# Where Q's block forms of x and V's first group of forms are made, in a fused cross-attention and expert kernel

## The chip, the core and the metric

The kernel runs on one NeuronCore of a Trainium2 chip. The metric is the device time of one execution in microseconds, median of several. TensorE (PE) multiplies matrices, VectorE (DVE), ScalarE (ACT) and GpSimd (POOL) work elementwise, SyncE (SP) issues the transfers here. GpSimd does not touch PSUM in this kernel.

## The reference

```python
def _layernorm(x): return (x - mean(x)) / sqrt(var(x) + 1e-5)

def xattn(h, ctx, mask, bias, ln_weight, w_q, w_k, w_v, w_out):   # 32 heads of 128
    x = rmsnorm(h) * ln_weight
    q, k, v = x @ w_q.T, ctx @ w_k.T, ctx @ w_v.T                 # 1024 x 512 @ 512 x 4096 each
    p = softmax(where(mask, q @ k.T + bias, -inf))                # per head and batch, 128 x 128
    return h + (p @ v) @ w_out.T

x = x + tanh(g_xattn) * xattn(layernorm(x), ctx_4096, ...)
x = x + tanh(g_ffn) * ffn(layernorm(x), ...)                      # base product, top 2 of 28 rank-8 experts
```

x and the context are 8 x 128 x 512 in float32.

## The kernel before

**Precision.** A float32 matrix is split into a rounded part `hi` (float32r, written by ScalarE, the "lead") and the rest `lo` = raw - hi (written by VectorE or GpSimd). Each product is three matmuls: hi x hi, hi x lo, lo x hi.

**Stages.** (1) The context is split, K and V of the first head pair are made, x is normalised and turned, and Q of the first pair is made. (2) `q_phase(0)` to `q_phase(14)`: Q of the other 15 head pairs. (3) V of the other 15 pairs, in four groups `g` of 4, 4, 4 and 3 pairs. (4) Attention over the pairs, with K made on the way. (5) The expert layer.

**Block products.** Stages 2, 3 and K use a scheme of 7 half-size products in place of 8. For Q the weights give the forms A11, A12, A22 (blocks as they are) and S1 to S4 (sums of blocks), x gives the blocks B11, B21, B22 and four forms T1 to T4, which are made once, before phase 0, and serve all 15 phases:

T1 = B12 - B11, T2 = B22 - T1, T4 = B21 - T2, T3 = B22 - B12.

In the code T1 to T4 are `t_raw[0]` to `t_raw[3]`. `t_form` on VectorE (line 1226) makes them, `lead_t` (854) rounds them on ScalarE, `rest_t` (1231) makes their rests on VectorE. The products of a phase stand on TensorE in this order: A11 B11; S1 T1; A12 B21; A22 T4; S2 T2; S4 B22; S3 T3. Each is 6 matmuls of 512 columns (line 1810). `post` on VectorE (1259) adds the products up; the seventh needs the post of the fifth, since it takes that bank again. `rest_a` (1236) makes the rests of A on VectorE; the sums S (`s_forms`, lines 600 to 605) and their rests (610) are GpSimd's.

**x before phase 0.** TensorE turns the eight row tiles of x into PSUM (`turn_xn`), ScalarE rounds each (`lead_xt`, 794), VectorE makes the rest (`rest_xt`, 1163), and ScalarE copies the raw tile to SBUF (`raw_xt`, 789). T1 needs both halves of x as raw copies, so VectorE waits for all eight (`xt_raw_done`).

**V's first group.** V's blocks of weights come in four raw slots R11, R21, R22, R12. Seven forms are rounded and multiplied in the order n = 0 to 6 by `v_product` (line 1885, 24 matmuls each, four row tiles of the context). The sums are made in the raw slots themselves:

```python
R11 = R11 - R21        # form 5         v_sums 1   DVE L1270
R21 = R21 + R22        # form 1         v_sums 2   DVE L1273
R21 = R22 - R11        # form 4         v_sums 3   POOL L700
R12 = R12 - R21        # form 3         v_sums 4   POOL L703
```

Form 1 lies where form 4 is written, so form 4 waits for form 1's rest, which is GpSimd's in the first group (`v_on_pool`), as is the rest of form 2 (line 685). The four forms of the context (`kt_raw`, differences at line 1279) are made during the last Q phases; GpSimd makes the rests of two (633, 639), VectorE of the other two (1324). After its sums GpSimd adds mask and bias (`add_mask(0)`, 574) and goes on to group 1. SP loads the blocks of group 1 when the rests of forms 3 to 6 are made.

Everything is a static order per engine with semaphores; each engine works its own list from the top.

## Time and profile before

| | |
|---|---|
| median of 3 runs | 848.75 us (848.27 to 848.85) |
| the profiled execution | 850.35 us, its span 848.6 us |
| busy: TensorE / VectorE / ScalarE / GpSimd | 821.9 / 594.8 / 380.5 / 442.6 us |
| mean granted TensorE clock | 0.991 of full |
| transferred | 145.48 MB, 171 GB/s on average |

The span runs from the first to the last instruction of the profiled execution. Busy time of TensorE includes modelled ends of pipelined matmuls, so starts are the better measure of its pace. In the timeline each row is one instruction or a run of like ones: start, time, engine, line, operation, tiles written and read; in brackets the idle time of the engine before it and what ended that.

### The profile page before, as it was taken

What the parts mean: (1) busy time and instruction counts of PE and PEld (TensorE: products, weight loads), DVE (VectorE), ACT (ScalarE), POOL (GpSimd) and SP (SyncE); (2) the same over time, 40 slices, a digit from 0 to 9 for tenths busy, and PEclk for the clock granted to TensorE, in tenths of its full rate; (3) what the DMA queues carried; (4) which work ended last, traced back from release to release, by engine and by line L of the source; (5) the groups of instructions that cost most, each with busy time, mean ns of one, the idle gap of its engine ahead of it and who ended that gap; (6) DMA issues with size and microseconds to landing.
All of it is one profiled execution on the core that took longest, in us unless ns stands there. A gap on an engine that the chain in (4) does not pass through costs nothing.

```text
span 848.6 us, 14325 instructions
## 1 busy us (share of the span) xinstructions
PE 821.9 (97%) x4270; PEld 702.8 (83%) x4270; DVE 594.8 (70%) x999; ACT 380.5 (45%) x1046; POOL 442.6 (52%) x406
## 2 busy tenths in 40 slices
PE   8979999999999999969999999999999999998998
PEld 6868888877788889858888888888888888887886
DVE  6886555767736354747887779777887788779852
ACT  5554444443433424443456344644555345642410
POOL 1365666676475473547545764477446754571200
PEclk9999999999999999969999999999999999999999
DMA  8228444543635554665665456555655566544001
GB/s 305 93 81 272 166 161 149 174 161 99 199 110 189 174 198 156 216 219 156 220 220 183 155 204 223 203 150 190 239 197 180 172 220 221 191 159 154 1 25 74
DMA packets 78556, 145.48 MB, mean 171 GB/s; under 512 B 7872, under 2 KB 44736, under 8 KB 76608
## 3 DMA queue, kind: packets, MB, share of 16 engines
q1 hardware_dynamic: 78528, 145.12, 50.7%
q8 instruction: 15, 0.25, 0.1%
q14 instruction: 13, 0.11, 0.1%
HBM read 94.77 MB, written 50.33 MB: 171 GB/s over the span
## 4 chain that ended last, share of the span: by engine, by line
PE 84%; DVE 6%; DMA 3%; issue 2%; POOL 2%; ACT 2%; SPq 1%; DVEq 0%; POOLq 0%; ACTq 0%
PE proj_ps L1810 16%; PE proj_ps L1618 13%; PE proj_ps L1866 12%; PE proj_ps L1885 7%; PE score_ps L1618 7%; PE proj_ps L1686 4%; PE score_ps L1885 4%; PE score_ps L1655 3%; PE proj_ps L2051 3%; PE turn_ps L1866 2%; PE pv_ps L1866 2%; PE pv_ps L1885 2%; PE turn_ps L1885 2%; PE score_ps L1686 2%; PE turn_ps L1655 2%
## 5 line engine op out<-in xcount | busy, mean ns | idle before, releaser
L574 POOL TENSOR_TENSOR comb<-mask_add,bias_sb 128x1024 f32<-128x1024 f32 x32 | 77.3, 2438 | 163.7 <-DVE attn L1380 163.7
L778 ACT ACTIVATE attn<-attn,neg_max 128x128 f32<-128x128 f32 x256 | 99.2, 391 | 34.9 <-DVE neg_max L1369 34.9
L984 ACT ACTIVATE w_hi<-w_raw 128x256 fp32r<-128x256 f32 x105 | 39.8, 413 | 102.9 <-POOL w_raw L648 70.0
L1402 DVE TENSOR_TENSOR acc<-proj_ps,acc 128x512 f32<-128x512 f32 x70 | 48.3, 689 | 37.3 <-PE proj_ps L1618 37.3
L658 POOL TENSOR_TENSOR w_lo<-w_raw,w_hi 128x256 fp32r<-128x256 f32 x105 | 73.4, 742 | 0.0
L610 POOL TENSOR_TENSOR w_lo<-w_raw,w_hi 128x256 fp32r<-128x256 f32 x60 | 47.4, 796 | 27.2 <-ACT w_hi L849 27.2
L1618 PE MATMUL proj_ps<-w_hi,tf_hi 128*128 128x512 f32 x156 | 61.1, 392 | 0.4 <-DVE tf_lo L1398 0.4
L1618 PE MATMUL proj_ps<-w_lo,tf_hi 128*128 128x512 f32 x156 | 60.7, 389 | 0.0
L1618 PE MATMUL proj_ps<-w_hi,tf_lo 128*128 128x512 f32 x156 | 60.7, 389 | 0.0
L1264 DVE TENSOR_TENSOR w_lo<-w_raw,w_hi 128x1024 fp32r<-128x1024 f32 (+1 forms) x20 | 28.2, 1426 | 41.0 <-ACT w_hi L884 41.0
L884 ACT ACTIVATE w_hi<-w_raw 128x1024 fp32r<-128x1024 f32 (+1 forms) x28 | 27.6, 1014 | 57.3 <-POOL w_raw L694 21.3
L563 POOL TENSOR_TENSOR w_lo<-w_raw,w_hi 128x1024 fp32r<-128x1024 f32 x20 | 47.6, 2387 | 8.1 <-ACT w_hi L758 8.0
L1686 PE MATMUL proj_ps<-attn,v_sb 128*128 128x128 f32 x376 | 46.5, 282 | 5.4 <-DMA attn<-block_spill 3.6
L1236 DVE TENSOR_TENSOR w_lo<-w_raw,w_hi 128x256 fp32r<-128x256 f32 x45 | 33.8, 755 | 25.4 <-ACT w_hi L844 25.2
L1686 PEld LDWEIGHTS proj_ps<-attn,v_sb 128*128 128x128 f32 x376 | 44.9, 198 | 5.7 <-DMA attn<-block_spill 3.7
L1398 DVE TENSOR_TENSOR tf_lo<-proj_ps,tf_hi 128x512 fp32r<-128x512 f32 x47 | 32.0, 690 | 24.0 <-ACT tf_hi L784 22.0
L778 ACT ACTIVATION_READ_ACCUMULATOR attn<-attn,neg_max 128x1 f32 x256 | 48.6, 190 | 0.0
L1380 DVE TENSOR_TENSOR attn<-attn,row_scale 128x512 f32<-128x512 f32 x64 | 44.3, 692 | 2.2
L1369 DVE TENSOR_REDUCE neg_max<-attn 128x4 f32<-128x512 f32 x64 | 43.9, 686 | 2.2
L849 ACT ACTIVATE w_hi<-w_raw 128x256 fp32r<-128x256 f32 x60 | 24.8, 417 | 42.0 <-PE proj_ps L1810 38.6
L685 POOL TENSOR_TENSOR w_lo<-w_raw,w_hi 128x1024 fp32r<-128x1024 f32 (+1 forms) x8 | 18.5, 2322 | 46.1 <-ACT w_hi L884 44.9
L1866 PE MATMUL proj_ps<-ct_hi,w_hi 128*128 128x512 f32 x90 | 36.8, 409 | 3.1 <-DVE tf_lo L1398 3.1
(326 smaller groups left out, 2542.4 us busy)
## 6 DMA issues: line engine op xcount, KB each, us to landing
w_raw<-in_weights SPq DMA_DIRECT2D x52, 512.0 KB, 5.5
v_sb<-v_spill SPq DMA_DIRECT2D x32, 512.0 KB, 3.7
q_spill<-attn SPq DMA_DIRECT2D x60, 256.0 KB, 3.0
qt<-q_spill SPq DMA_DIRECT2D x15, 1024.0 KB, 4.8
block_spill<-block_sb SPq DMA_DIRECT2D x30, 512.0 KB, 3.5
attn<-block_spill SPq DMA_DIRECT2D x120, 128.0 KB, 2.9
w_raw<-in_v_weights SPq DMA_DIRECT2D x12, 512.0 KB, 4.8
v_spill<-v_sb SPq DMA_DIRECT2D x12, 512.0 KB, 4.6
```

The costliest lines, as they stand in the source:

```text
L563: pool.tensor_tensor(lo, w_raw[:, k, :], hi.bitcast(F32), ALU.subtract).then_inc(w_lo_done[k], 1)
L574: pool.tensor_tensor(comb[:, j, :, :], mask_add[:, :, :], bias_sb[:, j:j + 1, :].to_broadcast([P, B, S]), ALU.add).then_inc(comb_done, 1)
L610: pool.tensor_tensor(columns(w_lo, WO, n), columns(w_raw, s_raw(i), n), columns(w_hi, WO, n).bitcast(F32), ALU.subtract).then_inc(qs_lo, 1)
L658: pool.tensor_tensor(columns(w_lo, slot, n), raw, columns(w_hi, slot, n).bitcast(F32), ALU.subtract).then_inc(k_lo, 1)
L778: e = act.activation(probs[:, u, i, :], probs[:, u, i, :], ACT.Exp, bias=neg_max[:, u, i:i + 1], accum_out=row_sum[:, u, i:i + 1])
L1380: dve.tensor_tensor(probs[:, u, :, :], probs[:, u, :, :], row_scale[:, u, :].unsqueeze(2).to_broadcast([P, BU, S]), ALU.mult).then_inc(pro ...
L1402: dve.tensor_tensor(acc[:, b, :], out_banks[b][:, :], acc[:, b, :], ALU.add).then_inc(acc_done, 1)
L1618: mm = pe.matmul(o, lhs(l, n), rhs(r, n), start=(start and n == 0 and m == 0), stop=(stop and n == terms - 1 and m == 2))
L1686: mm = pe.matmul(pv_bank(a, u)[:, i * S:(i + 1) * S], v_sb[:, b, j * DH:(j + 1) * DH], probs_t[:, t, :, j * BU + i, :], start=True, stop=True)
L1810: mm = pe.matmul(o[:, :], w[l][:, c, :], x[r][:, c, :], start=(start and c == 0 and m == 0), stop=(c == 1 and m == 2), skip_group_check=no ...
L1866: mm = pe.matmul(o[:, :], w[l][:, c, :], x[r][:, c, :], start=(start and c == 0 and m == 0), stop=(c == 1 and m == 2), skip_group_check=no ...
L1885: mm = pe.matmul(banks[m][:, 0:VN[g]], x[l][:, c, m * P:(m + 1) * P], w, start=(start and c == 0 and n == 0), stop=(c == 1 and n == 2), sk ...
```

## The change

**Q's forms of x.** `raw_xt` copies only the first four tiles (the first half of x). T1 and T2 are made tile by tile, four instructions of 128 x 256 each, with the second half of x read straight from the PSUM banks of `turn_xn`. T3 is rewritten from T2 - B11 and T4 from B21 - T2, both from SBUF and whole. T3's difference is made right behind the first rest of A, its lead goes in front of phase 0 on ScalarE. T1's rest goes in front of A's first rest. `T_DONE` holds the new counts.

**V's first group.** Form 1 gets a buffer of its own, `v_first_s1` (the first half of `block_sb`, free once the first context form's rest is made), so form 4 no longer waits for it. VectorE alone makes the sums and the rests of forms 0 to 4, in the order in which the products take them. GpSimd has nothing of group 0 left; its mask addition goes behind group 1's sums. On ScalarE the lead of the context form 1 goes one product earlier, V's form 1 behind the context form 3.

```diff
+T_DONE = (G, 2 * G, 2 * G + 2, 2 * G + 1)
...
+        def v_form_raw(g, n):
+            return v_first_s1 if g == 0 and n == 1 else v_raw(g, V_RAW[n])
+        def v_sum_at(g, n):
+            return g * SF + ({1: 1, 5: 2, 4: 3, 3: 4} if g == 0 else {5: 1, 1: 2, 4: 3, 3: 4})[n]
...
+        v_first_s1 = block_sb[:, 0, 0:2 * VN[0]]
...
         def v_on_pool(g, n):
-            return n == 1 or (n == 0 and g > 0) or (n == 2 and g == 0)
+            return g > 0 and n < 2
...
# GpSimd
             rest_kt(1, 2)
-            v_rest(0, 1)
-            v_rest(0, 2)
-            v_second_sums(0)
-            pool.wait_ge(kt_lo_done, TF)
-            pool.wait_ge(mask_done, 1)
-            add_mask(0)
             for g in range(1, VG):
                 v_rest(g, 0)
                 v_first_sums(g)
                 v_rest(g, 1)
                 v_last_sums(g - 1)
                 v_second_sums(g)
+                if g == 1:
+                    pool.wait_ge(kt_lo_done, TF)
+                    pool.wait_ge(mask_done, 1)
+                    add_mask(0)
...
# ScalarE
             copy_proj(0, UNITS + 4, 1, q_at(1))
-            for i in range(G, B):
-                raw_xt(i)
...
             lead_s(0, 0)
+            lead_t(0)
             copy_proj(0, UNITS + 5, 2, q_at(2))
-            lead_t(0)
+            lead_t(1)
             lead_s(0, 1)
             lead_s(0, 3)
             act.wait_ge(proj_done, PROJ0 - 1)
             lead_a(0, 0, 0, 0)
-            lead_t(1)
             lead_t(3)
             lead_a(0, 1, 0, 1)
-            lead_s(0, 2)
             copy_proj(0, UNITS + 6, 0, q_at(3))
             lead_a(0, 2, 1, 1)
+            lead_s(0, 2)
+            act.wait_ge(proj_done, PROJ0)
+            lead_t(2)
...
                 copy_product(i, s_copy, p1_ps)
+                if last:
+                    lead_kt(1, 3)
...
                 if first:
                     copy_proj(0, PROJ0 - 1, 3, v_dst(3))
                     lead_a(1, 0, 0, 0)
-                    lead_t(2)
...
                 if last:
-                    lead_kt(1, 3)
                     lead_kt(2, 3)
                     product(i, 4)
                     v_lead(0, 0)
-                    v_lead(0, 1)
                     product(i, 6)
                     lead_kt(3, 4)
+                    v_lead(0, 1)
                     product(i, 7)
                     v_lead(0, 2)
...
# VectorE
-            dve.wait_ge(xt_raw_done, B)
-            t_form(0, b_block(0, 1), b_block(0, 0))
-            dve.wait_ge(t_done, 1)
-            t_form(1, b_block(1, 1), t_raw[0])
-            dve.wait_ge(t_done, 2)
-            t_form(3, b_block(1, 0), t_raw[1])
+            dve.wait_ge(xt_raw_done, G)
+            for i in range(G, B):
+                t_tile(0, i, tile_ps(i, 0), tile_of(xt_raw[:, 0:2, :], i))
+            for i in range(G, B):
+                dve.wait_ge(t_done, i - G + 1)
+                t_tile(1, i, tile_ps(i, 1), tile_of(t_raw[0], i))
+            dve.wait_ge(t_done, 2 * G)
+            dve.tensor_tensor(t_raw[3], xt_raw[:, 2:4, half(0)], t_raw[1], ALU.subtract).then_inc(t_done, 1)
+            rest_t(0, 1)
             rest_a(0, 0, 0, 0)
-            rest_t(0, 1)
+            dve.tensor_tensor(t_raw[2], t_raw[1], xt_raw[:, 0:2, half(0)], ALU.subtract).then_inc(t_done, 1)
             rest_a(0, 1, 0, 1)
             rest_a(0, 2, 1, 1)
             rest_t(3, 3)
             rest_t(1, 2)
-            t_form(2, b_block(1, 1), b_block(0, 1))
             rest_t(2, 4)
...
+            def v_first_s1_sum():
+                dve.wait_ge(kt_lo_done, 1)
+                dve.wait_ge(vw_in[R21], 16)
+                dve.wait_ge(vw_in[R22], 16)
+                dve.tensor_tensor(v_first_s1, v_raw(0, R21), v_raw(0, R22), ALU.add).then_inc(v_sums, 1)
+            def v_first_group():
+                v_rest(0, 1)
+                ...
+                dve.tensor_tensor(v_raw(0, R11), v_raw(0, R11), v_raw(0, R21), ALU.subtract).then_inc(v_sums, 1)
+                ...
+                dve.tensor_tensor(v_raw(0, R21), v_raw(0, R22), v_raw(0, R11), ALU.subtract).then_inc(v_sums, 1)
+                v_rest(0, 2)
+                ...
+                dve.tensor_tensor(v_raw(0, R12), v_raw(0, R12), v_raw(0, R21), ALU.subtract).then_inc(v_sums, 1)
+                v_rest(0, 3)
+                v_rest(0, 4)
...
                 if last:
                     v_rest(0, 0)
-                    v_first_sums(0)
+                    v_first_s1_sum()
...
             q_phase(NQ - 1)
+            v_first_group()
...
# TensorE
-                v_product(g, 0, VB["11"], vx_ps, True, posted(g - 1, 13) if g else lambda m: pe.wait_ge(xt_raw_done, B))
+                v_product(g, 0, VB["11"], vx_ps, True, posted(g - 1, 13) if g else lambda m: pe.wait_ge(t_done, T_DONE[1]))
```

**First place: VectorE between the rests of x and phase 0's rests.** In these rows `comb` holds T1 and T2, `attn` the raw x with T3 and T4, `tf_lo` the rests of T1 and T2, and `w_lo<-attn` those of T3 and T4. Before:

```order
L1226 TENSOR_TENSOR comb<-attn 128x1024
L1226 TENSOR_TENSOR comb<-attn,comb 128x1024
L1226 TENSOR_TENSOR attn<-attn,comb 128x2x512
L1236 TENSOR_TENSOR w_lo<-w_raw,w_hi 128x256
L1231 TENSOR_TENSOR tf_lo<-comb,tf_hi 128x1024
L1236 TENSOR_TENSOR w_lo<-w_raw,w_hi 128x256 x2
L1231 TENSOR_TENSOR w_lo<-attn,w_hi 128x1024
L1231 TENSOR_TENSOR tf_lo<-comb,tf_hi 128x1024
L1226 TENSOR_TENSOR attn<-attn 128x2x512
L1231 TENSOR_TENSOR w_lo<-attn,w_hi 128x1024
L1236 TENSOR_TENSOR w_lo<-w_raw,w_hi 128x256 x2
```

After:

```order
L1235 TENSOR_TENSOR comb<-score_ps,attn 128x2x128 x2
L1235 TENSOR_TENSOR comb<-turn_ps,attn 128x2x128
L1235 TENSOR_TENSOR comb<-pv_ps,attn 128x2x128
L1235 TENSOR_TENSOR comb<-score_ps,comb 128x2x128 x2
L1235 TENSOR_TENSOR comb<-turn_ps,comb 128x2x128
L1235 TENSOR_TENSOR comb<-pv_ps,comb 128x2x128
L1255 TENSOR_TENSOR attn<-attn,comb 128x2x512
L1240 TENSOR_TENSOR tf_lo<-comb,tf_hi 128x1024
L1245 TENSOR_TENSOR w_lo<-w_raw,w_hi 128x256
L1258 TENSOR_TENSOR attn<-comb,attn 128x2x512
L1245 TENSOR_TENSOR w_lo<-w_raw,w_hi 128x256 x2
L1240 TENSOR_TENSOR w_lo<-attn,w_hi 128x1024
```

Two wide differences have become eight small ones that read PSUM, T1's rest stands in front of A's first rest, and T3's difference has moved from the last place but one to the place behind it.

**Second place: VectorE from the last Q phase to V's first group.** The rows with `proj_ps` are posts, `w_lo` rests of V's forms, `w_raw` and `block_sb` sums, `xt_lo` the context rests. Before:

```order
L1259 TENSOR_TENSOR attn<-proj_ps,lnw 128x512
L1264 TENSOR_TENSOR w_lo<-w_raw,w_hi 128x1024
L1270 TENSOR_TENSOR w_raw<-w_raw 128x1024
L1273 TENSOR_TENSOR w_raw<-w_raw 128x1024
L1259 TENSOR_TENSOR attn<-proj_ps,attn 128x512
L1259 TENSOR_TENSOR attn<-proj_ps,lnw 128x512
L1259 TENSOR_TENSOR attn<-proj_ps,attn 128x512
L1259 TENSOR_TENSOR attn<-attn 128x512
L1324 TENSOR_TENSOR xt_lo<-comb,xt_hi 128x2x512
L1324 TENSOR_TENSOR xt_lo<-block_sb,xt_hi 128x2x512
L1264 TENSOR_TENSOR w_lo<-w_raw,w_hi 128x1024 x4
```

After:

```order
L1275 TENSOR_TENSOR w_lo<-w_raw,w_hi 128x1024
L1282 TENSOR_TENSOR block_sb<-w_raw 128x1024
L1270 TENSOR_TENSOR attn<-proj_ps,attn 128x512
L1270 TENSOR_TENSOR attn<-proj_ps,lnw 128x512
L1270 TENSOR_TENSOR attn<-proj_ps,attn 128x512
L1270 TENSOR_TENSOR attn<-attn 128x512
L1275 TENSOR_TENSOR w_lo<-block_sb,w_hi 128x1024
L1289 TENSOR_TENSOR w_raw<-w_raw 128x1024
L1291 TENSOR_TENSOR w_raw<-w_raw 128x1024
L1275 TENSOR_TENSOR w_lo<-w_raw,w_hi 128x1024
L1295 TENSOR_TENSOR w_raw<-w_raw 128x1024
L1275 TENSOR_TENSOR w_lo<-w_raw,w_hi 128x1024 x2
```

The first sum is form 1's, in its own buffer; behind the posts follow the other sums and the rests of forms 1 to 4, and the two context rests come only then.

**The same place on GpSimd.** Before:

```order
L639 TENSOR_TENSOR xt_lo<-comb,xt_hi 128x2x512
L685 TENSOR_TENSOR w_lo<-w_raw,w_hi 128x1024 x2
L700 TENSOR_TENSOR w_raw<-w_raw 128x1024
L703 TENSOR_TENSOR w_raw<-w_raw 128x1024
L574 TENSOR_TENSOR comb<-mask_add,bias_sb 128x1024 x2
L685 TENSOR_TENSOR w_lo<-w_raw,w_hi 128x1024
L691 TENSOR_TENSOR w_raw<-w_raw 128x1024
L694 TENSOR_TENSOR w_raw<-w_raw 128x1024
```

After:

```order
L647 TENSOR_TENSOR xt_lo<-comb,xt_hi 128x2x512
L693 TENSOR_TENSOR w_lo<-w_raw,w_hi 128x1024
L699 TENSOR_TENSOR w_raw<-w_raw 128x1024
L702 TENSOR_TENSOR w_raw<-w_raw 128x1024
L693 TENSOR_TENSOR w_lo<-w_raw,w_hi 128x1024
L718 TENSOR_TENSOR attn<-attn,k_buf 128x512 x4
L708 TENSOR_TENSOR w_raw<-w_raw 128x1024
L711 TENSOR_TENSOR w_raw<-w_raw 128x1024
L582 TENSOR_TENSOR comb<-mask_add,bias_sb 128x1024 x2
```

Two rests and two sums of group 0 are gone, and the two mask additions (`comb<-mask_add,bias_sb`) stand behind group 1's sums.

## Rows read from the trace of the kernel before

**Rows 1.** The page, part 1: busy us (share of the span) xinstructions

```profile
PE 821.9 (97%) x4270; PEld 702.8 (83%) x4270; DVE 594.8 (70%) x999; ACT 380.5 (45%) x1046; POOL 442.6 (52%) x406
```

**Rows 2.** Waits of TensorE, 40 to 66 us: total us, times, longest

```profile
PE proj_ps L1810 <- DVE attn L1259: 3.4, 1, 3.4
```

**Rows 3.** The same view, 180 to 220 us

```profile
PE proj_ps L1885 <- DVE w_lo L1264: 1.7, 1, 1.7
...
PE proj_ps L1885 <- issue: 0.6, 1, 0.6
```

**Rows 4.** Timeline of TensorE: start us, us, engine line op tiles [idle before <-releaser]

```profile
47.00 0.28 PE L1618 MATMUL proj_ps<-w_lo,ct_hi 128*128 128x256 f32 x1
...
48.00 0.50 PE L1810 MATMUL proj_ps<-xt_hi,w_hi 128*128 128x512 f32 x1 [0.72 <-DVE w_lo L1236]
...
60.73 0.47 PE L1810 MATMUL proj_ps<-w_hi 128*128 128x512 f32 x1 [3.42 <-DVE attn L1259]
...
62.17 0.39 PE L1810 MATMUL proj_ps<-xt_hi,w_hi 128*128 128x512 f32 x1
...
196.43 0.42 PE L1885 MATMUL score_ps<-w_hi,ct_hi 128*128 128x512 f32 x1
...
221.07 0.39 PE L1885 MATMUL score_ps<-w_hi,xt_hi 128*128 128x512 f32 x1
```

**Rows 5.** Window sums: stretch, length, then PE, PEld, DVE, ACT, POOL, clock, DMA

```profile
61.00:185.00 124.00, 124.00 (x546) 102.03 (x544) 77.74 (x109) 57.38 (x130) 79.88 (x102) 1.00 0.54 181
```

**Rows 6.** Timeline of VectorE, 40 to 61 us

```profile
42.49 1.23 DVE L1226 TENSOR_TENSOR comb<-attn 128x1024 f32<-128x1024 f32 x1 [2.49 <-ACT attn L789]
...
52.48 1.75 DVE L1231 TENSOR_TENSOR tf_lo<-comb,tf_hi 128x1024 fp32r<-128x1024 f32 x1
...
58.17 1.81 DVE L1236 TENSOR_TENSOR w_lo<-w_raw,w_hi 128x256 fp32r<-128x256 f32 x2
...
60.51 0.41 DVE L1236 TENSOR_TENSOR w_lo<-w_raw,w_hi 128x256 fp32r<-128x256 f32 x1
```

**Rows 7.** Timeline of ScalarE, 45 to 50 us

```profile
45.89 0.42 ACT L844 ACTIVATE w_hi<-w_raw 128x256 fp32r<-128x256 f32 x1 [0.46 <-PE proj_ps L1618]
...
49.20 0.40 ACT L844 ACTIVATE w_hi<-w_raw 128x256 fp32r<-128x256 f32 x1
...
49.70 0.60 ACT L891 ACTIVATE lnw<-proj_ps 128x512 f32<-128x512 f32 x1
```

**Rows 8.** Timeline of GpSimd, 49 to 53 us

```profile
49.85 0.74 POOL L600 TENSOR_TENSOR w_raw<-w_raw 128x256 f32<-128x256 f32 x1 [0.17 <-POOL w_lo L610]
...
51.43 1.71 POOL L603 TENSOR_TENSOR w_raw<-w_raw 128x256 f32<-128x256 f32 x1
```

**Rows 9.** Timeline of VectorE, V's first and second group

```profile
194.01 0.69 DVE L1259 TENSOR_TENSOR attn<-proj_ps,lnw 128x512 f32<-128x512 f32 x1 [4.91 <-PE proj_ps L1810]
...
196.41 1.23 DVE L1270 TENSOR_TENSOR w_raw<-w_raw 128x1024 f32<-128x1024 f32 x1
...
203.01 3.42 DVE L1324 TENSOR_TENSOR xt_lo<-comb,xt_hi 128x1024 fp32r<-128x1024 f32 x1
...
251.45 1.23 DVE L1264 TENSOR_TENSOR w_lo<-w_raw,w_hi 128x1024 fp32r<-128x1024 f32 x1 [10.96 <-ACT w_hi L884]
```

**Rows 10.** Timeline of ScalarE, V's form 3

```profile
212.05 1.06 ACT L884 ACTIVATE w_hi<-w_raw 128x1024 fp32r<-128x1024 f32 x1 [8.15 <-POOL w_raw L703]
```

**Rows 11.** Timeline of GpSimd, V's groups

```profile
205.31 3.37 POOL L700 TENSOR_TENSOR w_raw<-w_raw 128x1024 f32<-128x1024 f32 x1
...
211.97 5.72 POOL L574 TENSOR_TENSOR comb<-mask_add,bias_sb 128x1024 f32<-128x1024 f32 x2
...
263.66 2.41 POOL L685 TENSOR_TENSOR w_lo<-w_raw,w_hi 128x1024 fp32r<-128x1024 f32 x1 [13.39 <-ACT w_hi L884]
```

**Rows 12.** w_raw between 186 and 204 us: loads (ns min/median/max, starts), landing

```profile
L339 SPq DMA_DIRECT2D w_raw<-in_v_weights x2: 400/1495/2590, 189.6 to 190.0; - x2
...
DMA to landing us min/median/max: 5.3/5.7/6.1
```

More of the change, by code:

```diff
@@ L1219, in _, with tile_ps, tile_of, t_tile @@
                 rest_xt(i, xt_hi_done, xt_lo_done, xn_ps)
-            def b_block(k, t):
-                return xt_raw[:, 2 * k:2 * k + 2, half(t)]
-            def t_form(n, l, r, op=ALU.subtract):
-                dve.tensor_tensor(t_raw[n], l, r, op).then_inc(t_done, 1)
+            def tile_ps(i, k):
+                return xn_ps[i % G][:, 2 * k * P:(2 * k + 2) * P].rearrange("p (c s) -> p c s", c=2)
+            def tile_of(raw, i):
+                return raw[:, :, (i - G) * P:(i - G + 1) * P]
+            def t_tile(n, i, l, r):
+                dve.tensor_tensor(tile_of(t_raw[n], i), l, r, ALU.subtract).then_inc(t_done, 1)
             def rest_t(n, place):
@@ L1336, in v_group @@
             def v_group(g):
-                for n in range(2 if g else 3, VFORMS):
+                for n in range(2 if g else 5, VFORMS):
                     v_rest(g, n)
```

29 lines of the change are left out of this document (13 added, 16 removed).

## The prediction

> **What bounds the kernel now.** I read the page first: TensorE is busy for 821.9 us of the 848.6 us span [rows 1]. So time can come only out of TensorE's gaps, and a change that touches VectorE, ScalarE and GpSimd is worth what it does to those gaps. Next I read who makes TensorE wait, in the two stretches that the diff touches. Around the first block phase of Q TensorE stands for 3.4 us and for 0.7 us, both times for VectorE [rows 2, 4]. Where V's first group begins it stands for 1.7 us behind a VectorE rounding rest and for 0.6 us that the view calls "issue" [rows 3]; that product waits for GpSimd's rest of form 1 by the code, so I count it as GpSimd's. Between the two, 546 matmuls fill 124.00 us without a gap, 0.227 us each, at the full granted clock [rows 5], so neither a clock step nor a hidden wait is to be had there.
>
> The modelled ends of matmuls hide part of a gap, so I price gaps by starts. First place: the last matmul of V's last row block starts at 47.00, the 256 columns cost 0.12 us, and phase 1 of Q starts at 62.17 [rows 4]. 42 matmuls of phase 0 need 42 x 0.227 = 9.5 us; 62.17 - 47.12 - 9.5 = 5.5 us are lost. Second place: V's first product starts at 196.43, the fifth at 221.07 [rows 4]. 96 matmuls need 21.8 us of the 24.64; 2.85 us are lost. The two places together, 8.4 us, are all that this change can win.
>
> **Part 1, Q's forms of x.** Before, VectorE idles 2.49 us before T1's difference at 42.49, because that waits for ScalarE's four copies of the second half of x; it had been free since 40.0 [rows 6]. Afterwards those four copies are gone (about 2 us of ScalarE, off the path) and T1 and T2 are built tile by tile from PSUM. That is 8 instructions of 256 elements. No such instruction is in the trace. The nearest is the 256-element rest of 0.41 us [rows 6]; back to back a start follows the last one some 0.08 us before its end, so 0.34 us each, 2.7 us in all, from 40.0 to 42.7. Bounds: 0.33 and, if each were as slow as in the blocked pair (1.81 us for two [rows 6]), 0.9 us, which would end at 47.1.
>
> Then T4's difference and T1's rest follow, wide ones of 1.23 us alone [rows 6], 1.14 us from start to start: done at 45.0. A11's rest now stands behind them, and its lead cannot begin before 45.89, when TensorE has read Q's old weights [rows 7]. Lead 0.42, rest 0.41: 46.75. TensorE is free at 47.12, so the 0.7 us wait goes.
>
> ScalarE's list from 45.89 to the copy at 49.70 is the same seven kinds of instruction as before (T3's lead in the place of T2's), so the copy that frees the first bank begins at 49.20 + 0.33 = 49.5 and ends at 50.1 [rows 7]. TensorE's third product could start at 49.85; it starts at 50.2, a new wait of 0.35 us. Its seventh product is then due at 50.2 + 4 x 1.36 = 55.65, against 60.73 before [rows 4].
>
> **What is late next** is VectorE. Between A11's rest and the seventh product it still has T3's difference, two rests of A, three rests of T, two rests of A for phase 1 and one addition. Alone that is 1.14 + 0.66 + 3.42 + 0.66 + 0.7 = 6.6 us, from 46.7 to 53.3, early enough. It isn't alone. A wide VectorE instruction at 52.48 took 1.75 us where an undisturbed one takes 1.23, and the GpSimd instruction beside it (256 wide, 51.43) took 1.71 where its fellows need 0.74 [rows 6, 8]: the two take turns, and each GpSimd instruction costs VectorE about 1.75 - 1.23 = 0.52 us. In this stretch GpSimd has the last rest of S, four sums for phase 1 and a rest, and five to six of them fall between: 3.0 us, an estimate from these rows. So the addition ends at 56.3 and the seventh product starts at 56.35. **Gain 60.73 - 56.35 = 4.4 us.** Bounds: 5.1 us if VectorE is not the limit (55.65), and 2.6 us if every instruction of that list is as slow as its blocked fellow before (1.7 wide, 0.9 narrow: 11.8 us from 46.3, 58.15). I take 4.4, because the count of GpSimd instructions is known and the 0.52 us is what the rows show for each.
>
> The Trainium skill's page "SBUF — State Buffer", section "Who interferes with whom", says that a VectorE instruction with two SBUF inputs and a GpSimd instruction that reads SBUF exclude each other for the whole of whichever starts first. Taken at its worst (VectorE always just too late, 0.74 us each, six times) it makes the loss 4.4 us, the seventh product 57.7 and the kernel 1.4 us slower than my number, an estimate by that page. By the same section an instruction with one input from PSUM is not in this at all; no row here shows eight such tiles beside GpSimd.
>
> **Part 2, V's first group.** All times here are of the old trace; the shift from part 1 moves every engine alike. Before, VectorE and GpSimd blocked each other: the two rests of KT took 3.42 us instead of 1.23 [rows 9], GpSimd's sum 3.37 us at 205.31 [rows 11], and ScalarE waited 8.15 us for the sum chain before it could make form 3 [rows 10]. Afterwards GpSimd has nothing ready after KT's second rest until group 1's data is in, so VectorE's wide instructions cost 1.23 us.
> - S1 into its own buffer needs R22. Its load is issued by 190.0 and lands at most 6.1 us later, 196.1 [rows 12]. Form 0's rest begins after the addition at 194.01 [rows 9] and ends at 195.9. S1: 196.1 to 197.35 (1.23 as at 196.41 [rows 9]). ScalarE leads it by 198.4 (1.06 [rows 10]).
> - Four additions of 0.61 us follow on VectorE, to 199.8; S1's rest is ready at 201.0. TensorE wants it at 196.43 + 24 x 0.227 = 201.87. Margin 0.9 us; the 0.6 us wait goes.
> - Two differences, form 2's rest, S4's difference: about 1.23 each, ready at 203.6, 204.8, 206.0. TensorE wants form 2 at 207.3: margin 2.5 us.
> - ScalarE's form 3 at 206.1 to 207.1, its rest at 208.3. TensorE wants it at 212.8. Margin 4.5 us; the 1.7 us wait goes.
> - What moves: lead of KT's form 1 goes one product earlier on ScalarE and delays one copy by 0.1 us with 3 us of room. The two KT rests come after form 4, at 211 to 214; they are first wanted after 223. SP's loads for group 1 hang on the rests of forms 3 to 6 and go out some 4 us earlier, so they cost nothing. The mask addition (two instructions, 5.72 us [rows 11]) goes behind group 1's sums. It then runs where GpSimd idled for 13 us, and may block group 1's form 3 on VectorE by 2.3 us, against a margin that I put at 2.9 us: before, this rest ended at 252.7 [rows 9], 1.0 us before TensorE wanted it (221.07 + 6 x 5.44 = 253.7), and the chain to it starts 4.5 us earlier now, TensorE only 2.7. So nothing, with an upper bound of 1 us.
>
> **Gain 2.85 us**; bounds 1.8 (that 1 us) and 2.85, since there is no more gap to take.
>
> **Sum.** 4.4 + 2.85 = 7.25 us. The profiled execution took 850.35 us around its span of 848.6; it would become 843.1 around 841.35. The median of the three runs is 848.75, 1.6 us below the profiled one, and gives 841.5. 0.2% (1.7 us) is about what a measurement tells from no change.
>
> **The rivals.**
> - *V's sums still come late.* VectorE does nine wide instructions one behind the other. If R22 lands late or the four additions wait, S1's rest misses 201.87. For it: the margin is only 0.9 us. Against it: all later margins are over 2 us. Only the first gain stays: 848.75 - 4.4 = 844.3. 8%.
> - *Q's gain is given back.* Phase 0 ends earlier, but the next weights, the ring of stores or GpSimd's sums don't, and a phase soon after waits. Against it: phases 1 to 12 ran without a gap on weights that came a phase ahead. 848.75 - 2.85 = 845.9. 8%.
> - *Blocking in both places, slower.* If GpSimd always had an instruction ready, all VectorE instructions of V's chain would cost 3.42 us like KT's rests [rows 9]. From 199.8: S1's rest at 203.2 (1.3 late), form 2's rest at 213.5 (4.9 more), form 3's at 221.4 (2.5 more), 8.7 us of gaps for 2.85, with 2.6 in part 1: 848.75 + 5.85 - 2.6 = 852.0. New gaps appear once a step takes over 1.9 us (7.5 us for four), and the whole turns slower from 2.9 us a step. Against it: GpSimd's list is empty there. 3%.
> - *It doesn't do what it says*: TensorE waits for another thing at both places, and nothing changes, 848.75. Every wait named has its releaser in the views. 3%.
>
> **The numbers.** The forecast, 841.5, has 78%. Its own ends are 4.4 to 8.4 us of gain (2.6 + 1.8 to all of both gaps), 844.4 to 840.35. The range 840.2 to 844.8 takes in the first rival and leaves out 14%. Faster by over 0.2%: 0.94; within: 0.03; slower: 0.03.
>
> **What would show it.** T1's first tile starts at about 39.9 and T2 ends by 43; TensorE's phase 0 starts at 47.1; its seventh product waits under 1 us for the same addition and starts at 56 to 56.7. VectorE's wide instructions between 190 and 210 (less the shift of 4.4) show 1.23 us and GpSimd none beside them; TensorE has no gap over 0.1 us from V's first product on. VectorE at 1.7 us or more there, or a gap in front of V's second product, would make the second part wrong; a seventh product after 57.5 the first.

## The result and the profile after

| | before | after |
|---|---|---|
| median of the runs, us | 848.51 (848.25 to 848.85, 4 runs) | 840.98 (840.78 to 842.29, 4 runs) |
| profiled execution, us | 850.35 (span 848.6) | 840.79 (span 839.0) |
| ratio after / before | | 0.9901, 95% interval 0.9888 to 0.9915 |

The change makes the kernel faster. The median after is 0.5 us under the forecast of 841.5; the ratio, which compares runs of one chip, makes the gain 8.4 us of 848.5 (7.2 to 9.5), where the two places were to give 7.25. A second comparison of the same kernel, `both` below, gave 0.9895. So the sign and the places came as forecast, and the gain is about 1 us more than the sum.

TensorE's busy time on the page answers to [rows 1]: 821.9 us became 819.3 us, while the span fell by 9.6.

```profile
PE 819.3 (98%) x4270; PEld 703.2 (84%) x4270; DVE 589.7 (70%) x1009; ACT 380.1 (45%) x1042; POOL 429.6 (51%) x402
```

TensorE's waits from 36 to 66 us after the change, in place of [rows 2]:

```profile
PE proj_ps L1644 <- DVE xt_lo L1169: 0.3, 1, 0.3
PE proj_ps L1836 <- ACT lnw L897: 0.2, 1, 0.2
```

And its timeline, in place of [rows 4]:

```profile
45.84 0.28 PE L1644 MATMUL proj_ps<-w_lo,ct_hi 128*128 128x256 f32 x1
45.96 0.40 PE L1836 MATMUL proj_ps<-xt_hi,w_hi 128*128 128x512 f32 x1
...
49.06 0.47 PE L1836 MATMUL proj_ps<-xt_hi,w_hi 128*128 128x512 f32 x1 [0.20 <-ACT lnw L897]
...
54.63 0.47 PE L1836 MATMUL proj_ps<-w_hi 128*128 128x512 f32 x1
...
56.10 0.39 PE L1836 MATMUL proj_ps<-xt_hi,w_hi 128*128 128x512 f32 x1
...
190.22 0.39 PE L1911 MATMUL score_ps<-w_hi,ct_hi 128*128 128x512 f32 x1
...
195.66 0.39 PE L1911 MATMUL proj_ps<-w_hi,xt_hi 128*128 128x512 f32 x1
...
211.98 0.39 PE L1911 MATMUL score_ps<-w_hi,xt_hi 128*128 128x512 f32 x1
```

Read by starts, as the prediction did. From V's last projection to phase 1: 56.10 - 45.84 - 9.65 = 0.6 us lost, 5.5 before. From V's first product to its fifth: 21.76 us for 96 matmuls, nothing lost, 2.85 before. That is 4.9 + 2.85 = 7.8 us. The remaining 1.8 us of the difference of spans lie in code that the change does not touch: the last projection began 1.16 us earlier, the fourteen phases between, 1 to 14, were 0.14 us shorter and all behind V's fifth product 0.5 us.

VectorE after the change, in place of [rows 6]:

```profile
39.74 0.42 DVE L1235 TENSOR_TENSOR comb<-pv_ps,attn 128x256 f32<-128x256 f32 x1
40.07 0.75 DVE L1235 TENSOR_TENSOR comb<-score_ps,comb 128x256 f32<-128x256 f32 x2
...
48.69 1.75 DVE L1240 TENSOR_TENSOR tf_lo<-comb,tf_hi 128x1024 fp32r<-128x1024 f32 x1
50.37 1.76 DVE L1240 TENSOR_TENSOR w_lo<-attn,w_hi 128x1024 fp32r<-128x1024 f32 x1
52.05 1.83 DVE L1245 TENSOR_TENSOR w_lo<-w_raw,w_hi 128x256 fp32r<-128x256 f32 x2
53.80 0.68 DVE L1270 TENSOR_TENSOR attn<-proj_ps,lnw 128x512 f32<-128x512 f32 x1
```

The reader sees the eight tiles at 0.33 us from start to start, T1 and T2 done at 41.5, and the addition for the seventh product done at 54.48, 0.15 us before TensorE starts it. VectorE and TensorE arrive together there. V's first group, in place of [rows 9]:

```profile
189.53 1.22 DVE L1282 TENSOR_TENSOR block_sb<-w_raw 128x1024 f32<-128x1024 f32 x1
...
193.19 1.22 DVE L1275 TENSOR_TENSOR w_lo<-block_sb,w_hi 128x1024 fp32r<-128x1024 f32 x1
194.33 1.22 DVE L1289 TENSOR_TENSOR w_raw<-w_raw 128x1024 f32<-128x1024 f32 x1
...
204.36 1.22 DVE L1349 TENSOR_TENSOR xt_lo<-comb,xt_hi 128x1024 fp32r<-128x1024 f32 x1
```

S1's rest ends at 194.4, 1.25 us before TensorE wants it at 195.66, and KT's rest takes 1.22 us instead of 3.42 [rows 9]. The mask addition, in place of [rows 11], and what it does to VectorE:

```profile
236.87 5.75 POOL L582 TENSOR_TENSOR comb<-mask_add,bias_sb 128x1024 f32<-128x1024 f32 x2
```

```profile
238.09 2.25 DVE L1275 TENSOR_TENSOR w_lo<-w_raw,w_hi 128x1024 fp32r<-128x1024 f32 x1 [7.23 <-ACT w_hi L890]
240.99 2.71 DVE L1275 TENSOR_TENSOR w_lo<-w_raw,w_hi 128x1024 fp32r<-128x1024 f32 x1 [0.64 <-ACT w_hi L890]
```

It blocks two rests by 1.0 and 1.5 us, and TensorE has no gap there: the margin of group 1 holds.

### The profile page after: what moved, and what is told of

Read it like the earlier page. It is cut to its first block, busy times and chain, and to the rows that moved or that the text cites. A ratio compares the mean times of both kernels' runs of the same rounds, so it can differ in the third digit from the quotient of the medians.

```text
span 839.0 us, 14328 instructions
## 1 busy us (share of the span) xinstructions
PE 819.3 (98%) x4270; PEld 703.2 (84%) x4270; DVE 589.7 (70%) x1009; ACT 380.1 (45%) x1042; POOL 429.6 (51%) x402
## 4 chain that ended last, share of the span: by engine, by line
PE 88%; DVE 3%; DMA 3%; issue 2%; ACT 2%; SPq 1%; POOL 1%; DVEq 0%; ACTq 0%; POOLq 0%
PE proj_ps L1836 17%; PE proj_ps L1644 13%; PE proj_ps L1892 12%; PE proj_ps L1911 8%; PE score_ps L1644 7%; PE score_ps L1911 5%; PE proj_ps L1712 4%; PE score_ps L1681 3%; PE proj_ps L2077 3%; PE pv_ps L1911 2%; PE turn_ps L1911 2%; PE turn_ps L1892 2%; PE pv_ps L1892 2%; PE score_ps L1712 2%; PE turn_ps L1681 2%
## 5 line engine op out<-in xcount | busy, mean ns | idle before, releaser
L693 POOL TENSOR_TENSOR w_lo<-w_raw,w_hi 128x1024 fp32r<-128x1024 f32 (+1 forms) x6 | 13.3, 2220 | 57.9 <-ACT w_hi L890 56.8
```

## The experiments

Gains are (1 - ratio) x 848.5 with their 95% interval. "Lost" is read by starts in the profile, at Q and at V's first group, as in the section above. The third column takes in what happens between the two places as well: it is the time from the start of the last matmul of V's last projection to the start of V's fifth product, 174.07 us in the first profile of the kernel before, less the same time in this profile; for the changed kernel itself it is 7.9 us. It rests on one profile of each kernel, and it differs between profiles of equal code, by 0.2 us between `both` and the first profile of the changed kernel and by up to 1.3 us for the kernel before.

| kernel | lost at Q / V, us | gain up to V's fifth product, us | gain measured, us |
|---|---|---|---|
| before_again | 6.25 / 2.9 | -1.3 | -0.1 (-1.2 to 1.0) |
| q_forms | 0.6 / 2.9 | 5.0 | 6.1 (4.8 to 7.3) |
| v_sums | 5.5 / 0 | 2.7 | 3.5 (2.1 to 4.8) |
| both | 0.6 / 0 | 7.8 | 8.9 (7.6 to 10.3) |
| q_order | 4.5 / 2.9 | 0.3 | 2.3 (1.4 to 3.3) |
| q_tiles | 4.7 / 2.9 | 0.5 | 0.6 (-0.3 to 1.5) |
| v_shared_slot | 0.6 / 0.5 | 7.2 | 8.2 (6.8 to 9.7) |
| kt_rest_later | 0.6 / 0 | 8.3 | 9.0 (7.5 to 10.6) |
| combined | 0 / 0 | 7.6 | 9.0 (7.6 to 10.4) |
| mask_first | 0.6 / 0 | 7.7 | 10.0 (7.6 to 12.4) |
| pool_writes | 0.6 / 0 | 7.6 | 8.3 (6.4 to 10.2) |
| pool_reads | 0.6 / 5.9 | 1.8 | 2.5 (1.4 to 3.6) |

The 6.25 us of `before_again` are 5.5 us of gaps and 0.7 us of a lower clock, which is taken up at the end of this section.

### The two parts alone

`q_forms` takes of the diff the hunks on T1 to T4 (the tiles, the lists of ScalarE and VectorE), `v_sums` those on V's first group.

> Part 1 alone: Q's forms of x are made as in the changed kernel, V's first group stays as before. Theory (the two places pay and add up): TensorE loses 0.6 us instead of 5.5 us between V's last projection and phase 1, and the 2.85 us at V's first group stay, so 848.5 - 4.9 = 843.6 us. Rival A, Q's gain is given back later: 848.5 with the gap somewhere behind phase 1. Rival B, there is a third gain that hangs on part 1: below 842.9.

> Part 2 alone: V's first group is summed by VectorE alone with its own buffer, Q's forms as before. Theory: only the 0.6 us and the 1.7 us waits at V's second and fourth products (2.9 us by starts) go, 848.5 - 2.9 = 845.6 us. Rival A, part 2 pays only since part 1 shifted the loads against it: a gap of over 0.5 us stays at V's first five products and the time is over 846.2. Rival B, a third gain hangs on part 2: below 845.0.

> The changed kernel itself, timed beside its two parts. Theory: the two gains add up, 848.5 - 7.8 = 840.7 us, and the sum of the two single gains agrees with it within 0.5 us. If the sum of the parts is short of it by 1 us or more, a gain beyond the two places exists. The start-up (first transfers of the context until V's last projection) should differ from run to run by about 1 us without regard to the kernel.

TensorE's gaps come out part by part as expected: each part removes its own place and leaves the other as it was. The measured gains add up within their intervals (6.1 + 3.5 = 9.6 against 8.9; the 0.5 us that I had allowed between them is finer than this comparison), so no coupling shows. Rival A of both falls. Each ratio is somewhat better than its gaps. That of `q_forms` gives 842.4 us, under the 842.9 of its rival B, a third gain that hangs on part 1, though its interval also holds the 843.6 of the theory; this is taken up below.

### Part 1: order or tiles

Both kernels are shown here against `q_forms`, so V's first group is as before in them. `q_order` keeps the new lists but makes T1 and T2 whole, from ScalarE's eight copies:

```diff
-            for i in range(G, B):
-                t_tile(0, i, tile_ps(i, 0), tile_of(xt_raw[:, 0:2, :], i))
...
+            dve.wait_ge(xt_raw_done, B)
+            dve.tensor_tensor(t_raw[0], xt_raw[:, 0:2, half(1)], xt_raw[:, 0:2, half(0)], ALU.subtract).then_inc(t_done, 1)
...
```

`q_tiles` keeps the tiles and puts the old lists of VectorE and ScalarE back (VectorE's shown):

```diff
-            rest_t(0, 1)
             rest_a(0, 0, 0, 0)
-            dve.tensor_tensor(t_raw[2], t_raw[1], xt_raw[:, 0:2, half(0)], ALU.subtract).then_inc(t_done, 1)
+            rest_t(0, 1)
...
             rest_t(1, 2)
+            dve.tensor_tensor(t_raw[2], t_raw[1], xt_raw[:, 0:2, half(0)], ALU.subtract).then_inc(t_done, 1)
```

> Part 1 with its new order of instructions on ScalarE and VectorE but without the tiles: ScalarE still copies all eight pieces of x, and T1 and T2 are whole differences of 1024 elements a partition that wait for the last copy. Theory (VectorE is the limit up to the seventh product): T1 starts at 42.5 as before instead of two to three us earlier, VectorE is behind the changed kernel by about 2.2 us there, the seventh product starts at about 58, and the kernel gains 2.7 us, 845.8. Rival (only the order matters, the tiles are hidden): 843.6, as part 1. Rival (only the tiles matter): 848.5.

> Part 1 with its tiles but the old order: T1 and T2 come tile by tile from PSUM and the four copies are gone, but A11's rest stands ahead of T1's rest again, T3 comes last on VectorE, and ScalarE's list is the old one. Theory (VectorE limited, old order costs a wait for Q's old weights at A11's rest before T1's rest can follow): the tiles alone bring 2.4 us of 848.5, 846.1, with a wait for VectorE left ahead of the seventh product. Rival (the order is worth nothing): 843.6, as part 1 alone. Rival (tiles are worth nothing without the order): 848.5.

Neither half is worth much alone: 1.1 and 0.8 us by the gaps at Q, 4.9 together. I had expected some 2.5 us of each. VectorE of `q_order` still waits for ScalarE's last copy:

```profile
42.08 1.22 DVE L1245 TENSOR_TENSOR comb<-attn 128x1024 f32<-128x1024 f32 x1 [2.50 <-ACT attn L790]
```

In `q_tiles` T2 is done at 41.7 as in the changed kernel, and VectorE then idles, because the rest of A11 stands first and TensorE has not yet read Q's old weights; T3, last in the list, holds up the rest behind it:

```profile
45.37 0.47 DVE L1238 TENSOR_TENSOR w_lo<-w_raw,w_hi 128x256 fp32r<-128x256 f32 x1 [2.43 <-ACT w_hi L843]
...
52.37 1.75 DVE L1255 TENSOR_TENSOR attn<-comb,attn 128x1024 f32<-128x1024 f32 x1
55.25 1.22 DVE L1233 TENSOR_TENSOR w_lo<-attn,w_hi 128x1024 fp32r<-128x1024 f32 x1 [1.13 <-ACT w_hi L853]
```

The tiles make VectorE free earlier, the order gives it something to do then. One without the other mostly moves the idle time.

In its one profile `q_order` also loses 0.8 us more than the kernel before in front of the seventh product of phase 2: the weights for phase 3 landed 6.3 us after their issue there, 5.5 us in the kernel before. That is why its third column has 0.3 us and not 1.1. The measured gain of 2.3 us lies above both numbers, and its interval leaves out both; this profiled execution was 1.1 us slower than the median of its runs. Why `q_order` is that much better in the timed runs than by its gaps stays open.

### V's sum without a buffer of its own

```diff
-                dve.tensor_tensor(v_first_s1, v_raw(0, R21), v_raw(0, R22), ALU.add).then_inc(v_sums, 1)
...
                 dve.tensor_tensor(v_raw(0, R11), v_raw(0, R11), v_raw(0, R21), ALU.subtract).then_inc(v_sums, 1)
...
+                dve.tensor_tensor(v_raw(0, R21), v_raw(0, R21), v_raw(0, R22), ALU.add).then_inc(v_sums, 1)
```

> The changed kernel without the buffer of its own for V's first sum: VectorE alone sums and rounds, but R11 - R21 has to come first and the sum then takes R21's place. Theory: one more wide instruction of 1.2 us ahead of the sum; the margin of S1's rest was 1.3 us in the changed kernel (it ended at 194.4, TensorE wanted it at 195.7), so the gap is 0 to 0.2 us and the time at most 0.2 us above the changed kernel's. Rival (the buffer is what pays): S1 comes 1 us or more late and the time is 1 us or more above the changed kernel's.

The sum starts at 191.22 instead of 189.53, and V's second product starts 0.61 us after the matmul before it instead of 0.23; with the next step 0.5 us are lost, more than the 0.2 expected and less than the rival's 1 us. The timed runs, 840.0 to 841.8 us, cannot be told from those of the changed kernel. What pays in part 2 is that VectorE does this group alone; the buffer is worth 0.5 us of its 2.9.

### GpSimd beside VectorE

Both kernels add work on a scratch buffer that computes nothing; `pool_writes` has 20 memsets in the loop instead of 8 additions:

```diff
             rest_kt(1, 2)
+            pool.memset(busy_sb[:, :], 0.0).then_inc(busy_done, 1)
+            for n in range(8):
+                pool.wait_ge(busy_done, n + 1)
+                pool.tensor_tensor(busy_sb[:, :], busy_sb[:, :], busy_sb[:, :], ALU.add).then_inc(busy_done, 1)
```

> The changed kernel with one memset and 8 additions of 896 elements a partition on GpSimd, all on a scratch buffer in SBUF, behind KT's second rest, where GpSimd is otherwise idle; they compute nothing. Theory (the two engines take turns for the whole of an instruction): VectorE's wide instructions there, 1.22 us in the changed kernel, take 2.5 us or more each while the additions last, S1's rest is over 3 us late, and the whole kernel is 5 us or more slower than the changed one. Rival (each GpSimd instruction costs VectorE 0.52 us, as at the first Q phase): 8 x 0.52 = 4.2 us in all against margins of 1.3 us, so 1 to 3 us slower. Rival (no blocking): 1.22 us each and no change.

> The changed kernel with 21 memsets of 896 elements a partition on GpSimd at the same place: it is as busy but reads no SBUF. Theory (it is the reading of SBUF that makes the two engines take turns): VectorE's wide instructions stay at 1.22 us and the time stays within 0.5 us of the changed kernel's. Rival (any GpSimd instruction takes its turn): VectorE's take over 1.5 us each, and the kernel is over 2 us slower.

The timeline of `pool_reads`, VectorE first, GpSimd below:

```profile
194.78 0.69 DVE L1276 TENSOR_TENSOR attn<-proj_ps,attn 128x512 f32<-128x512 f32 x1
195.39 2.01 DVE L1276 TENSOR_TENSOR attn<-attn 128x512 f32<-128x512 f32 x1
197.32 2.70 DVE L1281 TENSOR_TENSOR w_lo<-block_sb,w_hi 128x1024 fp32r<-128x1024 f32 x1
199.94 2.70 DVE L1295 TENSOR_TENSOR w_raw<-w_raw 128x1024 f32<-128x1024 f32 x1
```

```profile
188.16 18.63 POOL L726 TENSOR_TENSOR busy_sb<-busy_sb 128x896 f32<-128x896 f32 x8
```

Two of these eight by themselves, one that no two-input SBUF instruction of VectorE held up and one between VectorE's wide ones:

```profile
188.16 1.68 POOL L726 TENSOR_TENSOR busy_sb<-busy_sb 128x896 f32<-128x896 f32 x1
...
199.01 2.54 POOL L726 TENSOR_TENSOR busy_sb<-busy_sb 128x896 f32<-128x896 f32 x1
```

and of `pool_writes`:

```profile
194.77 1.22 DVE L1281 TENSOR_TENSOR w_lo<-block_sb,w_hi 128x1024 fp32r<-128x1024 f32 x1
```

```profile
188.70 18.08 POOL L726 MEMSET busy_sb<- 128x896 f32 x20
```

GpSimd is busy for 18 us in both. Reading, it slows VectorE's wide instructions to 2.62 us from start to start (1.14 alone); only writing, not at all. The theory holds and both rivals fall, and it shows what part 2 has to keep away from VectorE: 8 reading instructions put back here cost 5.9 us at V's group (up to 1.7 of it by the clock, see below) and 6.4 us of measured time against `both`. An addition with one input in PSUM (194.78) keeps its 0.69 us beside the same GpSimd work, one with both in SBUF (195.39) takes 2.01, 0.68 in the changed kernel.

The two engines take turns for nearly the whole of an instruction, in three sizes. This addition of 896 elements takes GpSimd 1.68 us undisturbed, and 1.14 + 1.68 = 2.82 for 2.62 measured. KT's two rests before, 203.01 and 206.35, start 3.34 us apart, for 1.14 + 2.40 = 3.54 with the 2.40 us of an undisturbed GpSimd rest of 1024 (185.37 in `mask_first`). At Q two rests start 1.68 us apart (48.69 and 50.37), for 1.14 + 0.74 = 1.88 with an undisturbed GpSimd instruction of 256 (44.62). Each time the pair is 0.20 us shorter than the sum.

The Trainium skill's page "SBUF — State Buffer", section "Who interferes with whom", states the exemptions, for one PSUM input and for a GpSimd instruction that only writes; both traces agree. Its other rule, in the section "SBUF: two separate sides", is that whichever starts first holds the shared ports for its whole instruction and the other is blocked. The three pairs agree with it to within those 0.20 us.

### The place of the mask addition

```diff
             rest_kt(1, 2)
+            pool.wait_ge(kt_lo_done, TF)
+            pool.wait_ge(mask_done, 1)
+            add_mask(0)
```

> The changed kernel with the mask addition on GpSimd ahead of group 1's sums, as it stood before, in place of behind them. Theory (its place is free): within 0.3 us of the changed kernel, since GpSimd sits idle there for 28 us until group 1's data. Rival (two instructions of 5.7 us block VectorE's wide rests of V's first group or KT): a gap at one of V's products and 1 us or more slower. Rival (behind the sums it does harm now): 0.7 us or more faster.

It ran at 208.4, since it waits for VectorE's last KT rest, and took 5.75 us. Two rests of V there took 5.41 us together instead of 2.36, and TensorE has no gap. By the gaps its place is free, as forecast; the measured 10.0 us has an interval (7.6 to 12.4) too wide to say more.

### Two attempts at more

`kt_rest_later`, on GpSimd:

```diff
-            pool.tensor_tensor(kt_form_at(1, 0), kt_raw[0], kt_form_at(0, 0).bitcast(F32), ALU.subtract).then_inc(kt_lo_done, 1)
             q_phase(NQ - 2)
+            pool.tensor_tensor(kt_form_at(1, 0), kt_raw[0], kt_form_at(0, 0).bitcast(F32), ALU.subtract).then_inc(kt_lo_done, 1)
```

`combined` has in addition, on ScalarE, `lead_t(2)` behind `copy_product(i, s_copy, p1_ps)` of phase 0, and on VectorE phase 1's first two `rest_a` behind `post(i, 5, ...)`.

> The changed kernel with one move: GpSimd's wide rest of KT's form 0 stands behind its work for the last Q phase but one, so that it does not run beside VectorE's context difference. Theory (turn-taking of the two engines costs TensorE the 0.3 and 1.0 us waits for VectorE's additions ahead of V's group): these waits shrink and the time falls by 0.5 us against the changed kernel. Rival (the waits come from TensorE's own order): no change. Rival on the other side (the rest comes late for KT's first product): slower by 0.8 us or more.

> kt_rest_later plus a change ahead of Q's seventh product: T3's lead moves behind the copy that frees the first bank, and phase 1's two rests of A move behind the addition for the seventh product. Theory: the waits of 0.2 us at the third product and 0.2 to 0.3 us at the seventh go, 0.4 us more than kt_rest_later gives. Rival (moving the rests of A makes phase 1's first products wait): no faster than the changed kernel, with a wait for w_lo in phase 1.

The context difference on VectorE, in the changed kernel and then in `kt_rest_later`:

```profile
172.66 3.42 DVE L1303 TENSOR_TENSOR block_sb<-block_sb,comb 128x1024 f32<-128x1024 f32 x1
```

```profile
172.97 1.22 DVE L1303 TENSOR_TENSOR block_sb<-block_sb,comb 128x1024 f32<-128x1024 f32 x1
```

In `kt_rest_later` the view of TensorE's waits shows none from 56 to 190 us, and the two slow starts before V's group, 0.73 and 0.34 us, are 0.23: 0.6 us are gained in the trace. The comparison, 9.0 us against 8.9, is too coarse to confirm it. In `combined` phase 0 runs without any gap, 0.6 us more, but at the sixth and seventh product of phase 2 it loses 1.5 us, where `kt_rest_later` loses 0.4. TensorE's waits in `combined` (in `kt_rest_later` the view has none), and ScalarE's first lead for phase 3, in `kt_rest_later` and then in `combined`:

```profile
PE proj_ps L1841 <- DVE attn L1271: 0.8, 1, 0.8
...
PE proj_ps L1841 <- ACT attn L895: 0.3, 1, 0.3
```

```profile
70.70 0.42 ACT L848 ACTIVATE w_hi<-w_raw 128x256 fp32r<-128x256 f32 x1 [2.74 <-DMA w_raw<-in_weights]
```

```profile
72.49 0.42 ACT L848 ACTIVATE w_hi<-w_raw 128x256 fp32r<-128x256 f32 x1 [3.94 <-DMA w_raw<-in_weights]
```

The start-up, which no edit touches, put `combined` 1.05 us behind; the rest of the 1.8 us between the two leads is a real delay, and ScalarE waits 1.2 us longer for the weights. Their load was issued at nearly the same time in both, 65.05 and 65.34 us, but it landed 5.6 us later in the one and 7.1 us later in the other. What had moved is the load before it, of phase 2's weights: it fills the buffer that the moved rests read, so it went out at 57.33 instead of 54.94 us, 1.3 us more than the start-up explains, and the stores and context loads behind it followed later. That phase 3's weights landed late because of this fuller queue is argued and not shown. A gain is given back two phases later, the mechanism of the prediction's second rival. I count `combined` as no improvement over `kt_rest_later`.

### Where the extra microsecond comes from

> The kernel before, timed against itself, to see how far two sets of runs of one kernel lie apart. The changed kernel's measured gain (8.4 to 8.9 us by its two ratios) is above the 7.8 us that the two places lost, and so are those of its parts. Theory (only spread): the ratio is 1.000 within 0.001, and its profile shows the same waits at the two places, 5.5 us and 2.9 us, while the start of V's last projection and the waits for data near 366 us differ from the first profile by about 1 us. Rival (the comparison favours the kernel that is tried): a ratio under 0.999.

The ratio of the kernel before to itself is 1.0001 (0.9988 to 1.0014), so the comparison favours nobody. But its profile shows what the first one did not. The gap in front of the seventh product, 3.8 us from start to start, is followed by a lower clock:

```profile
60.68 0.47 PE L1810 MATMUL proj_ps<-w_hi 128*128 128x512 f32 x1 [3.40 <-DVE attn L1259]
...
62.01 0.63 PE L1810 MATMUL proj_ps<-w_hi,w_lo 128*128 128x512 f32 x1
62.43 0.63 PE L1810 MATMUL proj_ps<-w_lo,w_hi 128*128 128x512 f32 x1
```

In window sums of the same profile (the third figure from the end is the granted clock):

```profile
60.60:65.00 4.40, 4.32 (x12) 3.48 (x13) 2.73 (x5) 0.42 (x1) 0.79 (x2) 0.61 0.61 179
65.00:70.00 5.00, 5.00 (x24) 4.13 (x23) 3.73 (x5) 3.13 (x7) 4.06 (x5) 1.00 0.77 214
```

Matmuls start 0.43 us apart instead of 0.23 from 61.3 to 64.7 us: 1.2 GHz instead of 2.4. From the start of the seventh product to the thirteenth matmul from there, at 65.09, it takes 4.41 us instead of 2.8, so 1.6 us are lost beyond the gap. Four more profiles asked how often.

> One more profile of the kernel before. Theory (the 3.8 us gap between two products of Q's phase 0 sometimes makes the granted clock fall to half for some 3 us behind it, as in one of four profiles so far): in some of these looks the matmuls behind the gap start 0.43 us apart in place of 0.23, in others not. Rival (the fall is not tied to the gap): no look shows it there, or falls show at places without a gap before 345 us.

> As look_1: a second profile of the kernel before, on the same chip.

> A second profile of the kernel with tiles in the old order, which keeps the 3.8 us gap. Theory: it is like the kernel before in this, the fall shows in some profiles and not in others; the gap itself is 3.8 us again. Rival: never here.

> A second profile of the kernel with 8 additions on GpSimd. Theory: the gap of about 3.7 us between V's first and second product is there again, and the fall of the clock behind it, seen in its first profile, can be there or not. Everywhere else before 345 us the matmuls start 0.23 us apart.

`look_1` and `look_2` are the kernel before, `look_3` is `q_tiles`, `look_4` is `pool_reads`. `look_1` and `look_3` show the fall behind the same gap, `look_2` does not. Of the seven profiles that have the 3.8 us gap, three show it (before_again, look_1, look_3) and four don't (the first of before, v_sums, q_tiles, look_2). `pool_reads` and `look_4`, with a gap of 3.7 us at V's second product, both show it there:

```profile
196.44 0.39 PE L1917 MATMUL pv_ps<-w_lo,ct_hi 128*128 128x512 f32 x1
200.11 0.70 PE L1917 MATMUL proj_ps<-w_hi,xt_hi 128*128 128x512 f32 x1 [3.29 <-issue]
200.61 0.63 PE L1917 MATMUL proj_ps<-w_hi,xt_lo 128*128 128x512 f32 x1
201.04 0.63 PE L1917 MATMUL proj_ps<-w_lo,xt_hi 128*128 128x512 f32 x1
```

There it cost 1.7 us in the one and 2.9 us in the other, up to the last matmul of V's second product. No profile of a kernel without such a gap shows matmuls 0.43 us apart between 60 and 340 us, and the 2.1 us gap in front of V's fourth product, in eight profiles, never has it behind it.

So the gap had a second price. Not all of the 1.6 us stays lost: the three profiles with a fall do not have the short slow start at the seventh product of phase 2 (0.39 to 0.63 us in the four without). Up to V's fifth product the profiles with a fall are 1.0 to 1.3 us longer than those of the same kernel without one: 175.3 and 175.4 us against 174.1 and 174.3 for the kernel before, 174.6 against 173.6 for `q_tiles`. In the mean the second price is 3/7 x 1.1 = 0.5 us, an estimate from few profiles. The four profiles of the kernel before have 174.8 us in the mean, the two of the changed kernel (its first and `both`) 166.2: a difference of 8.5 us, where the first pair gave 7.9 and the timed runs 8.4 and 8.9.

The timed runs point the same way, but cannot name the place. Each lists its mean granted clock. The means by kernel are 0.9908 to 0.9917 where the 3.8 us gap stands (the kernel before in four comparisons, `before_again`, `v_sums`, `q_tiles`), 0.992 to 0.995 where it is gone (the changed kernel, `q_forms`, `v_shared_slot`, `kt_rest_later`, `combined`, `mask_first`, `pool_writes`), and 0.9938 for `q_order`, where the gap is 1.5 us. But every one of the eighteen profiles has another fall between 355 and 380 us, behind waits for data: from 345 to 400 us the granted clock is 0.88 in eleven, 0.91 in five and 0.94 in two, and it differs between two profiles of the changed kernel (0.88 and 0.94). A part of the difference in the mean clock, and of the extra time, may lie there.

With 0.5 us more the gains up to V's fifth product become 8.3 us for both (measured 8.4 and 8.9) and 5.5 for q_forms (6.1), and stay at 2.7 for v_sums (3.5) and 0.5 for q_tiles (0.6), all inside their intervals; q_order's 0.8 is outside (2.3, from 1.4). For both, q_forms, v_sums and q_tiles the value without the 0.5 us is inside too, so no single comparison shows the clock's share. That the fall occurs behind this gap, and what it costs there, is shown; that it makes up the whole of the extra gain is argued.

The Trainium skill's page "TensorE: Matmul & The Clock Gate", Part 1, says that a monitor of TensorE's activity halves its clock after it has been idle, and knows only the two levels. The rows agree in both: behind a gap matmuls start 0.23 or 0.43 us apart. Why the same gap brings the fall in one execution and not in another, no run here shows.

## Why the prediction was right, and where it was not

- **What bounds the kernel.** Right. TensorE's gaps at the two places make up 7.8 of the 9.6 us by which the two spans differ, the rest lies in code that no edit touches, and the rival that nothing changes is out.
- **Part 1, the tiles.** Forecast 0.34 us each, 2.7 in all; measured 0.33 and 2.8 (38.75 to 41.5). The bound of 0.9 us each was far off.
- **Part 1, the start of phase 0 and the third product.** In the time of the old trace (add the 1.16 us by which the last projection shifted) phase 0 started at 47.12 without a wait, the third product at 50.22 for 50.2, waiting for the copy as named.
- **Part 1, VectorE.** This term was mis-sized. I took 3.0 us of blocking by five to six GpSimd instructions of 0.52 us each. The price of one was right, the count was not: four of them held VectorE up, for 0.52 and 0.53 us at the two wide rests and 1.1 us in the pair at 52.05. They are those at 47.57, 49.53, 51.12 and 52.68; the fifth, at 53.56, stood beside an addition with an input in PSUM, which kept its 0.68 us. With 0.2 us in the pair before, where GpSimd was idle, the list took 2.35 us more than alone. The addition ended at 55.64 in the old time, not 56.3, and the seventh product started at 55.8, not 56.35. Gain 4.9 instead of 4.4, inside the bounds of 2.6 and 5.1. (The lower bound's 11.8 us does not come out of its own prices: from A11's rest on they give 12.0, behind it 11.1, so 58.3 or 57.8 for 58.15. Nothing hangs on it.) The estimate of 57.7 by the Trainium skill's page "SBUF — State Buffer", section "Who interferes with whom", took six instructions at 0.74 us each; the rows show four at 0.52 to 0.54 us.
- **The pieces of part 1.** Not forecast, and wrong in the expectations: order and tiles were priced as if each had its own gain. They have one together.
- **Part 2.** Forecast 2.85, measured 2.88. The margin in front of S1's rest was 1.25 us for 0.9; R22 landed in time, no wide instruction took over 1.23 us, GpSimd had none beside them. Its first rival, with the 0.9 us margin as its ground, did not happen.
- **The mask addition at nothing.** Right. It blocked by 1.0 and 1.5 us, less than the 2.3 allowed, and `pool_reads` shows what blocking does where there is no margin.
- **Slower by blocking in both places.** As a mechanism right, as an event not: in `pool_reads`, at 2.62 us a step, it gave 5.9 us at V's group, more than the 3.8 us that this rival's chain gives at that step (an estimate by its own sums); V's first sum and one addition were blocked too, and the clock fell. The whole kernel was still 2.5 us faster than before. No run reached the 2.9 us a step from which it was to be slower.
- **The sum and the low end.** The step that failed is the statement that "the two places together, 8.4 us, are all that this change can win", and with it the low end of the range, 840.2 us. It priced a gap at its own length, with nothing for the clock behind it, from one profiled execution in which the clock stood at 1.00 there. In three of seven profiles it falls, which costs 1.6 us on the spot and 1.0 to 1.3 us up to V's fifth product. Of the 1.15 us by which the measured gain of 8.4 exceeds the sum of 7.25, 0.5 are the VectorE term, and the other 0.65 are about the size of the clock's share, an estimate of 0.5 us; that they are the same is argued. By the ratio the changed kernel lies at 840.1 us (839.0 to 841.3), just outside the range; by its median, 840.98, inside. A trace of one execution cannot rule out what happens in three of seven.
